# Attention's window on TensorE: which sums are stored when, which tiles are projected when, and in which array shape

## The reference

```
x = x + xattn(ctx, layernorm(x))      # queries from x (1024), keys and values from context and x
x = x + moe(layernorm(x))             # one shared expert and the best two of eight
# xattn, per batch b and head h (16 heads of 64):
xn = layernorm(ctx) * g_x + b_x;  ln = layernorm(layernorm(x)) * g_l + b_l
q = ln @ Wq;  k, v = [xn; ln] @ Wkv            # 77 + 1024 keys
sim = (rmsnorm(q) * gq / 8) @ (rmsnorm(k) * gk).T    # masked where the context is masked
out = softmax(sim) @ v;  return out @ Wout + bout
```

## Time and profile before

| | |
|---|---|
| time, median of 3 runs | 2611.41 us (2608.67 to 2623.45) |
| profiled execution | 2611.24 us, its span 2609.4 us |
| engines' busy shares of the span | TensorE 94%, weight loads 77%, VectorE 70%, ScalarE 65%, GpSimd 46% |
| windows 0 to 31 of the attention | from about 100 us to 1790 us |
| output projection, then experts | to about 1960 us, then to the end |

### The profile page before, as it was taken

The page is one execution under the profiler, slowest core; times in us unless marked ns, Lnnn a source line. Parts: engine busy times, 40 slices in busy tenths (PEclk is TensorE's granted clock), DMA queues, the critical chain, the costliest instruction groups (busy, mean ns, idle before and its releaser), DMA issues. The chain is left out here.

```text
span 2609.4 us, 53706 instructions
## 1 busy us (share of the span) xinstructions
PE 2445.7 (94%) x19926; PEld 1999.6 (77%) x19926; DVE 1817.0 (70%) x2452; ACT 1695.8 (65%) x2286; POOL 1190.8 (46%) x783
## 2 busy tenths in 40 slices
PE   4899999999999999999999999986989999999997
PEld 3677777777777777677767767655989999999997
DVE  7667766776677666776677667765876566777775
ACT  2678787887788778877887778873333334444443
POOL 4334433453344334443344334422533526666676
PEclk8899999999999999999999999998989999999999
DMA  6323232323332323223233323145731459999996
GB/s 195 138 80 110 95 98 79 121 80 98 92 114 82 100 88 110 86 96 100 86 111 95 88 86 113 46 119 121 171 94 67 147 166 320 321 321 317 323 322 172
DMA packets 231533, 363.26 MB, mean 139 GB/s; under 512 B 59559, under 2 KB 139739, under 8 KB 227400
## 3 DMA queue, kind: packets, MB, share of 16 engines
q1 hardware_dynamic: 204694, 301.66, 37.7%
q0 software_dynamic: 25696, 58.82, 7.8%
q10 hardware_dynamic: 978, 0.34, 0.1%
HBM read 280.90 MB, written 79.85 MB: 138 GB/s over the span
## 5 line engine op out<-in xcount | busy, mean ns | idle before, releaser
L831 ACT ACTIVATE pr_hi<-ps_s 128x1024 fp32r<-128x1024 f32 x512 | 527.3, 1030 | 246.7 <-PE ps_s L975 186.5
L721 DVE TENSOR_TENSOR pr_lo<-ps_s,pr_hi 128x1024 fp32r<-128x1024 f32 x416 | 504.2, 1218 | 240.7 <-ACT ps_s L832 240.7
L1011 PE MATMUL ps_o<-pr_hi,vA 64*65 64x512 f32 x2036 | 437.3, 399 | 64.9 <-DVE o_first L652 48.9
L463 POOL TENSOR_TENSOR rs<-ss,minus_half 128x16 f32<-128x16 f32 (+1 forms) x96 | 225.6, 2350 | 488.6 <-DVE ss L696 488.6
L1011 PE MATMUL ps_o<-pr_lo,vA 64*65 64x512 f32 x2036 | 430.8, 392 | 0.0
L1011 PE MATMUL ps_o<-pr_hi,vC 64*65 64x512 f32 x2036 | 430.0, 391 | 0.0
L1685 ACT ACTIVATE ht<-f_ps_h,b 128x256 f32<-128x256 f32 x440 | 184.4, 471 | 340.1 <-PE f_ps_h L1617 282.1
L721 DVE TENSOR_TENSOR pr_lo<-pr,pr_hi 128x1024 fp32r<-128x1024 f32 x160 | 288.2, 1816 | 159.5 <-ACT pr L832 154.8
L832 ACT ACTIVATE ps_s<-ps_s 128x1024 f32<-128x1024 f32 x384 | 395.4, 1030 | 0.0
L461 POOL TENSOR_TENSOR sq<-raw 128x1024 f32<-128x1024 f32 (+1 forms) x96 | 165.8, 1727 | 429.5 <-ACT raw L776 429.5
L1617 PE MATMUL f_ps_h<-xT_hi,w 128*128 128x256 f32 x1760 | 355.2, 285 | 2.8 <-DVE xT_lo L1719 2.3
(11 more groups left out here) (220 smaller groups left out, 4676.2 us busy)
## 6 DMA issues: line engine op xcount, KB each, us to landing
w<-w1S_dram SPq DMA_DIRECT2D x160, 512.0 KB, 6.9
lnT_sb<-lnT_dram SPq DMA_DIRECT2D x31, 2304.0 KB, 9.0
w2raw<-in_L_ffn_Wproj SPq DMA_DIRECT2D x78, 512.0 KB, 7.1
w1S_dram<-cut POOLq DMA_DIRECT2D x36, 512.0 KB, 3.0
rec<-rden_dram SPq DMA_DIRECT2D x63, 256.0 KB, 3.7
routed_dram<-empty POOLq DMA_DIRECT2D x28, 387.0 KB, 3.6
xt<-routed_dram SPq DMA_DIRECT2D x39, 258.0 KB
w_raw<-in_L_xattn_Wkv SPq DMA_DIRECT2D x66, 128.0 KB, 2.9
```

The costliest lines, as they stand in the source:

```text
L463: g.tensor_tensor(rs[:, 0:sums], ss[:, 0:sums], minus_half[:, 0:sums], ALU.pow).then_inc(s_pool, 1)
L721: v.tensor_tensor(pr_lo[:, ring(w, d), :], full_of(d), pr_hi[:, ring(w, d), :].bitcast(F32), ALU.subtract).then_inc(s_lo, 1)
L831: act.activation(pr_hi[:, ring(w, d), :], ps_s[:, d % 2, :], ACT.Exp, bias=bias)
L1011: ins = mm(ps_o[0:DH + 1, h, :], v_[rows, h], p_[rows, 512 * h:512 * h + 512], start=k == 0 and part == 0 and i == 0, stop=k == KT - 1 and ...
```

## The change

Five edits in the attention, whose arithmetic stays as it is. (1) `divide` of group 1 goes from unit 9 to unit 12, and in SP's order `spread` of group 0 goes ahead of `store` of group 1. (2) Tiles 0 to 3 are projected as two 64-row twos in units 6 and 8; tile 4 alone stays whole, in unit 11; `squares` of the first group goes from unit 14 to 12. (3) The ninth tile's turn goes from unit 6 to unit 11. (4) Unit 11 gets the form of unit 2: `second(11)`, `fresh(12)`, that turn, tile 4, and the values of units 9 and 10 whole; in unit 13 `first` goes ahead of the second part of the projection. (5) `SPARED` becomes 0, 1, 9, 10: unit 10's whole probabilities now go to SBUF, those of units 16 and 17 stay in PSUM. The waits are renumbered to fit (`turn_job`, `tile_job`, `ready`); GpSimd's first and third group now wait each for the turns that read what they write over.

```diff
@@ -75,12 +75,13 @@
 MOST = 70.0
 PARTS = (("k", 0, 4), ("q", 0, 4), ("k", 4, 8), ("q", 4, 8), ("k", 8, 9))
 TURNS = len(PARTS)
-TURNED = {2: (0, 1), 4: (2, 3), 6: (4,)}
-PROJECTED = {6: (0,), 8: (1, 2), 11: (3, 4), 13: (5, 6), 15: (7, 8)}
-HALVED = (8, 13, 15)
-BETWEEN = 11
-WHOLE = 2
-SPARED = (0, 1, 9, 16, 17)
+TURNED = {2: (0, 1), 4: (2, 3), 11: (4,)}
+PROJECTED = {6: (0, 1), 8: (2, 3), 11: (4,), 13: (5, 6), 15: (7, 8)}
+HALVED = (6, 8, 13, 15)
+OPENED = (2, 11)
+WHOLE = [q + e for q in (0, KT) for e in range(2)]
+AHEAD = 4
+SPARED = (0, 1, 9, 10)
 JOBS = TURNS + KT
 PREP = [(c, g) for g in range(2) for c in range(C)] + [(c, None) for c in range(C)]
 PREPS = len(PREP)
@@ -252,6 +253,14 @@
             ring = (pr_hi, pr_lo)[part]
             return ring[:, :, :].rearrange("p r n -> p (r n)")[:, c * KEYS:c * KEYS + KEYS]
 
+        def turn_job(w, i):
+
+            return w.n(JOBS, JOBS + KT + (i if i < AHEAD or not w.proj else i + AHEAD) + 1)
+
+        def tile_job(w, tile):
+
+            return w.n(JOBS, JOBS + KT + AHEAD + (tile if tile < AHEAD else tile + 1) + 1) if w.turn else tile + 1
+
         def place(j):
 
             c, g = PREP[j]
@@ -374,9 +383,9 @@
                 if w.first:
                     sp.wait_ge(p_lnT, 192)
                 if w.attend:
+                    spread(w, 0, 0)
                     if not w.first:
                         store(w, 1, 1)
-                    spread(w, 0, 0)
                     broadcast(w, 0, 0)
                     if closing(w) and w.s == 1:
                         store(w, 0, 0)
@@ -456,8 +465,8 @@
                 n_, tiles, j0 = stop - first, slice(first, stop), 2 if first == NT else 0
                 qk, sums = raw[:, tiles, j0 * DH:4 * DH], (4 - j0) * n_
                 pool.wait_ge(s_raw, w.n(KT, 2 * KT + stop))
-                if k == 0:
-                    wait(pool, s_job, w.n(JOBS, JOBS + KT + TURNS) if w.turn else 0)
+                if w.turn and k != 1:
+                    pool.wait_ge(s_job, turn_job(w, TURNS - 1 if k else AHEAD - 1))
                 g.tensor_tensor(sq[:, 0:n_, j0 * DH:], qk, qk, ALU.mult).then_inc(s_sq, 1)
                 pool.wait_ge(s_ss, w.n(2 * GROUPS, 4 * GROUPS + 2 * k + 2))
                 g.tensor_tensor(rs[:, 0:sums], ss[:, 0:sums], minus_half[:, 0:sums], ALU.pow).then_inc(s_pool, 1)
@@ -723,8 +732,8 @@
                         if w.attend and not w.first:
                             if d == 5:
                                 invert(w, 1, 1)
-                            if d in (7, 9):
-                                divide(w, (d - 7) // 2, 1)
+                            if d in (7, 12):
+                                divide(w, (d - 7) // 5, 1)
                         if w.attend and d == 13:
                             invert(w, 0, 0)
                         if closing(w) and w.s == 1 and d == 16:
@@ -734,8 +743,8 @@
                                 turned(w, i)
                         if w.turn and d in (3, 5):
                             values(w, d == 5)
-                        if w.proj and d in (14, 17):
-                            squares(w, (d - 14) // 3)
+                        if w.proj and d in (12, 17):
+                            squares(w, (d - 12) // 5)
                         if closing(w) and w.s == 1 and d in (4, 6, 9, 11):
                             lower(d)
                         if d == 2 and not (isinstance(w.v, int) and (w.v == -1 or 2 * w.v + w.s == WINDOWS - 1)):
@@ -756,7 +765,7 @@
                 kind, first, stop = PARTS[i]
                 cols = slice(first * P, stop * P)
                 src = ps_m[:, (1 + i) % 2, 0:cols.stop - cols.start]
-                act.wait_ge(s_job, w.n(JOBS, JOBS + KT + i + 1))
+                act.wait_ge(s_job, turn_job(w, i))
                 if kind == "k":
                     act.activation(k_hi[:, w.other, cols], src, ACT.Copy).then_inc(s_thi, 1)
                 else:
@@ -764,13 +773,10 @@
 
             def projected(w, tile):
 
-                if w.turn:
-                    act.wait_ge(s_job, w.n(JOBS, JOBS + KT + TURNS + tile + 1))
-                    if tile == 0:
-                        act.wait_ge(s_v, w.n(2, 4))
-                        act.wait_ge(s_nrm, w.n(GROUPS, 2 * GROUPS))
-                else:
-                    act.wait_ge(s_job, tile + 1)
+                act.wait_ge(s_job, tile_job(w, tile))
+                if w.turn and tile == 0:
+                    act.wait_ge(s_v, w.n(2, 4))
+                    act.wait_ge(s_nrm, w.n(GROUPS, 2 * GROUPS))
                 bank = tile % 2
                 lo = 0 if tile < NT else PW
                 act.activation(raw[:, tile, lo:], ps_m[:, bank, lo:3 * PW], ACT.Copy).then_inc(s_raw, 1)
@@ -898,6 +904,8 @@
                 at = 2 if kind == "k" else 0
                 if i < 2:
                     pe.wait_ge(s_raw, w.n(KT, 2 * KT - 1 + i))
+                elif i == AHEAD and w.proj:
+                    pe.wait_ge(s_raw, w.n(KT, 2 * KT + AHEAD))
                 else:
                     pe.wait_ge(s_tlo, w.n(TURNS, TURNS + i - 1))
                 pe.wait_ge(s_nrm, w.n(GROUPS, GROUPS + -(-stop // MOST_TILES)))
@@ -909,9 +917,11 @@
             def ready(w, tile):
                 if tile < 2:
                     if w.turn:
-                        pe.wait_ge(s_tlo, w.n(TURNS, 2 * TURNS + tile - 1))
+                        pe.wait_ge(s_tlo, w.n(TURNS, TURNS + AHEAD - tile))
                 else:
                     pe.wait_ge(s_raw, w.n(KT, 2 * KT + tile - 1))
+                    if w.turn and tile == AHEAD + 1:
+                        pe.wait_ge(s_tlo, w.n(TURNS, 2 * TURNS))
                 if not w.turn and tile % 4 == 0:
                     pe.wait_ge(p_split, tile + 4)
                 if tile == 0:
@@ -1004,7 +1014,7 @@
                 if part == 0:
                     begin(w, d, g, k)
                 else:
-                    pe.wait_ge(s_half, w.n(UNITS - WHOLE, d + 1 if d < 0 else d + 1 - WHOLE))
+                    pe.wait_ge(s_half, w.n(UNITS - len(WHOLE), d + 1 - sum(e < d for e in WHOLE)))
                 for i, (v_, p_) in enumerate(pairs):
                     for t in range(2):
                         h, rows = t ^ swap, slice(DH * t, DH * t + DH)
@@ -1025,7 +1035,7 @@
                                 project(w, tile)
 
                     def second(d):
-                        if w.attend and not (w.first and d < LAG + 1):
+                        if w.attend and not (w.first and d < LAG + 1) and d - LAG - 1 not in WHOLE:
                             values_half(w, d - LAG - 1, 1, d % 2)
 
                     def first(d):
@@ -1047,29 +1057,28 @@
                             scores(w, d, general)
 
                     for d in range(UNITS):
-                        if d != 3:
+                        if d - 1 not in OPENED:
                             fresh(d)
                         if w.proj and d in HALVED:
                             project_halves(w, HALVED.index(d), PROJECTED[d], 0)
                             second(d)
+                            if d - LAG in OPENED:
+                                first(d)
                             project_halves(w, HALVED.index(d), PROJECTED[d], 1)
-                            first(d)
-                        elif d == 2:
+                            if d - LAG not in OPENED:
+                                first(d)
+                        elif d in OPENED:
                             second(d)
-                            fresh(3)
+                            fresh(d + 1)
                             jobs(d)
                             if w.attend:
-                                pe.wait_ge(s_v, w.n(2, 2))
-                                for e in range(WHOLE):
-                                    values(w, e)
-                        elif d == BETWEEN:
+                                if d == LAG:
+                                    pe.wait_ge(s_v, w.n(2, 2))
+                                for e in range(2):
+                                    values(w, d - LAG + e)
+                        elif d - 1 not in OPENED:
+                            jobs(d)
                             second(d)
-                            jobs(d)
-                            first(d)
-                        elif d != 3:
-                            jobs(d)
-                            if d != 4:
-                                second(d)
                             first(d)
                         if isinstance(w.v, int) and w.v == -1:
                             opening(w, d)
```

## The result

Over four runs of each the changed kernel takes 2509.11 us (2508.05 to 2512.38), the kernel before 2612.98 (2608.67 to 2623.45). The ratio is 0.9599, with a 95% interval of 0.9569 to 0.9629. The forecast was 2564 and its range began at 2540: the direction was right and the gain more than twice what I gave it. The two profiled executions, 2611.24 and 2512.38, differ by 98.9 us, their spans by 98.6.

What follows compares the result with a forecast made beforehand. TensorE, busy 94% of the span, was taken as the bound. From 2611 us, 37 came off over windows 1 to 29 (15 x 1.9 + 14 x 0.6) and 10 in the last windows: 2564, range 2540 to 2602.

Steps and rivals of the forecast that it cites:

- cover of 0.8 us: Unit 11: VectorE's copy of the first group's sums ends 0.8 us before TensorE comes to the values of unit 9.
- The stretch of unit 11: TensorE from the end of `second(11)` to the scores of unit 13: 7.04 us becomes 5.24, 1.8 less a window.
- The hold of unit 1's `pr_lo`: Unit 1, alternate windows: GpSimd's multiplication into `nrm` starts first, `pr_lo` ends 1.3 us late, nearly all passed to TensorE.
- Rival (a): No window has unit 1's `pr_lo` held behind GpSimd: 2546 us, chance 0.20.
- +0.46 - 0.52: Per window: units 5 to 6 lose 0.46 us to halves and a wait; sparing other units gains 0.52.
- the 0.32 of unit 5: TensorE's wait for `pr_lo` before unit 6's scores, 0.32 us a window, goes once VectorE is ahead.
- 1.86: Gain in us of a window in which unit 1's `pr_lo` is not held, said as 1.9; 0.6 if held.
- The late windows: Last windows: five waits total 16.2 us, 5.3 already in the sum; of the other 11, 10 us taken as gain.
- (b): Unit 1's `pr_lo` is held behind GpSimd in every window: 2584 us, chance 0.17.
- (c): VectorE's chain from unit 1 to 6 eats unit 11's gain; only late windows gain: 2601 us, chance 0.10 with (e).
- (d): VectorE held twice between units 1 and 6, at `pr_lo` and `vC`, with longer waits: slower, 2645 us, chance 0.08.
- (e): Copy in unit 10 comes no sooner because `ps_o` isn't done: time of (c), chance 0.10 shared with it.

Runs made afterwards that it cites:

- e1: Kernel before with only group 1's division moved from unit 9 to 12 and SP spreading group 0 ahead of storing group 1: 2548.12 us.
- e2: Changed kernel with group 1's division back in unit 9 and SP's store of group 1 again ahead of the spread of group 0: 2574.20 us.
- e9: Kernel before with the changes of e1 and e4 together, projection, turns and form of unit 11 as before: 2515.92 us.
- e4: Kernel before with units 16 and 17 no longer spared, nothing else changed: 2583.07 us.
- e3: Changed kernel with units 16 and 17 spared again, their whole probabilities in SBUF: 2502.18 us.
- e12: e3 with VectorE's squares of tiles 0 to 3 back in unit 14 instead of 12: 2548.36 us.
- e5: Changed kernel with tiles 0 and 1 projected whole in unit 6, not as 64-row twos: 2513.69 us.
- e11: e3 with `second(6)` ahead of the first halves in unit 6, and squares of tile 8 moved from unit 2 to unit 4: 2617.15 us.
- e6: Changed kernel with unit 1 no longer spared: 2634.88 us.
- e13: Changed kernel with VectorE's copy of group 1's sums moved behind `pr_lo` of unit 1: 2510.33 us.

## Why the prediction was wrong in size

**Edit 1: right, and the larger part.** The wait for `o_first` and its cause were read correctly; e1 removes them alone for 64.7 us, e2 brings them back for 65. Of the cover of 0.8 us 0.5 was there (the copy ends at 980.67, the values start at 981.21), and between 200 and 1500 us no TensorE row waits for the copy.

**The stretch of unit 11: the step that failed first.** The term was -1.80. Up to the scores of unit 13 it is 4.92 - 7.04 = -2.12, for turn and tile with both changes of the array took 981.21 - 979.85 = 1.36, not 1.69 and 0.1. Of the 1.69, taken from unit 6, some 0.27 was no work but the wait of tile 0 for `q_lo`, which ends at 1006.34; transpose and tile start 0.35 apart there and 0.08 in unit 11 after:

```profile
1006.04 0.33 PE L905 MATMUL ps_m<-a_ident,nrm 128*128 128x128 f32 x1
1006.39 1.31 PE L928 MATMUL ps_m<-w_sb,lnT_sb 128*128 128x384 f32 x6
```

And the term stopped too early. I compared "units 9 and 10's values halves" before with "twelve whole values matmuls" after, as if both were the same work. Before, three of the four halves lie ahead of 1027.88; the fourth, three groups or 0.69 us, was in unit 13, from 1029.63:

```profile
1029.63 0.40 PE L1011 MATMUL ps_o<-pr_hi,vA 64*65 64x512 f32 x2
...
1032.08 0.39 PE L975 MATMUL ps_s<-q_hi,k_hi 64*128 64x512 f32 x2
```

After, all four are inside the whole matmuls, and unit 13 has one less. The next stretch, scores of 13 to scores of 14, went from 4.20 (1027.88 to 1032.08) to 3.62. Over both the change is 8.54 - 11.24 = -2.70. One thing makes my term too large: the window that I read had a wait of 1.36, the mean is 1.06, so a mean window had 10.94 there and the change is -2.40. That is 0.60 more than my term, 19 us over 31 windows. e9 shows how it divides: with edit 1 and without edits 2 to 4 the two stretches take 9.45 (1029.30 to 1038.75). The 0.9 that these edits then take out of units 11 to 13 they put back elsewhere in the window, since the period stays at 50.10.

**The hold of unit 1's `pr_lo`: not there.** The term of +1.3 in 14 windows, 18 us, rested on the multiplication starting first and the subtraction waiting. The meeting took place as computed, but GpSimd was the one held. A window with the short power, VectorE then GpSimd:

```profile
1003.86 1.22 DVE L661 COPY o_second<-ps_o 65x1024 f32<-65x1024 f32 x1 [0.99 <-PE ps_o L1021]
1005.00 1.21 DVE L730 TENSOR_TENSOR pr_lo<-pr,pr_hi 128x1024 fp32r<-128x1024 f32 x1
```
```profile
1004.35 3.63 POOL L474 TENSOR_TENSOR nrm<-raw,rs 128x1024 f32<-128x1024 f32 x1
```

The multiplication starts in the record 0.65 us before the subtraction and ends at 1007.98, 1.8 after the subtraction's end, about the 1.90 that it takes alone: it ran second. Rival (a) had this result for another reason. The alternation of 1.3 us that I asked for isn't there; neighbouring periods differ by 0.02.

**Edits 2, 3 and 5 in units 16 to 6: near.** I had +0.46 - 0.52 = -0.06; the rest of the period says -2.59 + 2.40 = -0.19. Both subtractions take 1.22, and the small waits at the scores of unit 1 and before tile 0 are there. Edit 5 alone gave 0.58 a window in e4, but that this is near my 0.52 is luck: with the 0.32 of unit 5, which I booked under edits 2 and 3, I gave it 0.84, and it brings 0.95 in e4's undisturbed windows and 1.05 behind edit 1. Its given reason, that the operand in PSUM makes the subtraction short, was not what the changed kernel needed, since edit 2 had already moved GpSimd's squares away (e3, e12). That edits 2 to 4 bring nothing in the steady windows as a whole is shown by e9; what each brings is shown only for the halving in unit 6 (e5, 0.16).

**Counts.** The gain is in 31 periods, not 29 (2 x 1.9 = 4 us). The late windows gave 14.5, not 10, and the tail 4, which I had left out; what made the tail shorter was not looked into. A part of the late loss was the clock: the kernel before waited in one of them

```profile
1502.16 0.69 PE L1011 MATMUL ps_o<-pr_hi,vA 64*65 64x512 f32 x2 [3.91 <-DVE o_first L652]
```

and had the low level then, for 6.8 us, and in two other places, from 1712.9 and from 1764.1:

```profile
1501.20:1508.00 6.80, 5.84 (x28) 4.09 (x30) 4.08 (x4) 1.94 (x2) 0.00 (x0) 0.50 0.19 40
```

The kernel after has none between 103 and 1693 us. I priced those waits at their length alone. With 19 for unit 11, 18 for the hold, 4 for units 16 to 6 (0.13 x 31), 4 for the two periods, 4.5 and 4.2, less 1 for having rounded 1.86 up to 1.9, this is 53 for the 52 us (98.9 - 47) by which I was short.

Rivals (b), (c), (d) and (e) are excluded by the rows above. Two mechanisms of (d) exist at other places, though: a chain through GpSimd made late by an edit on VectorE (e11), and waits of TensorE that grow past what was removed (e6); e11 and e6 were both slower than the kernel before.

## What to carry to other kernels

Draw the boundary of a term where both kernels have done the same work, and count every matmul on both sides; a stretch that ends at the same instruction is not the same work once the order has changed. Take it from a mean window: the one that I read had 0.3 us more of the wait than the others. A removed wait has to be followed to the next one: edit 5 gave nearly half of its worth back until edit 1 had taken the wait behind it. A mean period can hide a few windows that went otherwise. Before an instruction is moved later, look up what stands behind it in order on the other engine: two units cost 122 us where the slack was 2.2 us a window.

## What the runs showed of the hardware

**Who gets the port.** A VectorE subtraction with both operands in SBUF and a GpSimd multiplication or square of 128x1024 exclude each other (e12). Where VectorE was idle, the one that started first won: 967.02 against 967.27. Where VectorE's subtraction stood ready behind a running copy, it won although GpSimd's multiplication had started 0.65 us before it in the record (1004.35 against 1005.00). The Trainium skill, "SBUF — State Buffer", section "SBUF: two separate sides", says that whichever starts first holds the shared pair for the whole instruction. The exclusion and the whole instruction agree with e12; the order agrees there and not at 1004.35, where the measurement decides. Whether it is the place in VectorE's queue that decides was not isolated. A GpSimd record that starts too early can't alone explain it, since a lead of 0.25 won and one of 0.65 lost. A copy from PSUM (e6, e13) does not take part: the multiplication beside it took 1.90 and 1.91.

Not every GpSimd instruction keeps VectorE out. A power that started 0.27 us ahead of a subtraction with both operands in SBUF left it at 1.23, in the changed kernel:

```profile
1001.37 2.90 POOL L472 TENSOR_TENSOR rs<-ss,minus_half 128x16 f32<-128x16 f32 x1 [5.78 <-DVE ss L705]
```
```profile
1001.64 1.23 DVE L730 TENSOR_TENSOR pr_lo<-pr,pr_hi 128x1024 fp32r<-128x1024 f32 x1 [0.35 <-issue]
```

The other way round it is held: 3.83 instead of 2.90 where the subtraction started first.

**A wait of TensorE can cost more than its length.** Waits of 2.5 us (e6) and 2.7 us (e11) in an otherwise full stretch went with some 3 us at a granted clock of 0.5 (1.2 GHz), which cost another 1.6 us, in 19 and in 16 of 23 steady periods. With shorter waits it was rarer, but not absent. In e2 the granted clock fell at the waits of 2.69 and 2.90 us and at none of the other 23 (1.10 to 1.81). In e4 it fell at the wait of 3.9 us and at three of 1.49 to 1.51, one of them here, and not at one of 1.56; the kernel before had 24 waits of 0.8 to 1.6 between 200 and 1495 us and kept 1.00.

```profile
960.64 0.45 PE L1011 MATMUL ps_o<-pr_hi,vA 64*65 64x512 f32 x2 [1.49 <-DVE o_first L652]
```
```profile
962.00:965.40 3.40, 3.40 (x20) 2.02 (x18) 1.13 (x2) 1.94 (x2) 0.00 (x0) 0.51 0.07 13
```

Which windows were spared, and why, stays open.
